# Half of a chunk's decay factors from stored rows instead of a matmul, in a one-core state-space kernel

## The reference, cut to what matters

```python
zxbcdt = hidden_states @ in_proj_w.T            # 1024 tokens, 512 -> 18560
xBC = silu(causal_conv4(zxbcdt[..., DIN:DIN + CONV_DIM]))   # x, B, C
dt = softplus(dt + dt_bias); Adt = -exp(A_log) * dt
L = exp(segment_sum(Adt))                       # exp of differences of running sums, 0 above the diagonal
Gm = einsum('bcihn,bcjhn->bhcij', C, B)
Y_diag = einsum('bhcij,bcjhd->bcihd', Gm * L, xs)
states = ...                                    # carried from chunk to chunk with exp(A_cumsum)
y = (Y_diag + Y_off + D * x) * silu(gate)
y = rmsnorm_by_group(y) * norm_w                # 8 groups of 1024 channels
x = x + y @ out_proj_w.T + ffn(layernorm(x))
```

## Time and profile before

| | |
|---|---|
| median of 3 runs | 1941.55 us (1940.65 to 1942.32) |
| profiled execution | 1946.74 us, span of its instructions 1945.0 us |
| mean granted clock of TensorE | 0.993 |
| PE / PEld busy | 97% / 76% of the span |
| DVE / ACT / POOL busy | 75% / 60% / 49% |
| cells with tiles | 60 of 64, mean length 25.8 us (328.86 to 1876.21 us) |

### The profile page before, as it was taken

How to read it: one execution, slowest core, us unless ns; L and a number is a source line. 1 busy time by engine, 2 the same in 40 slices (tenths; PEclk the granted TensorE clock), 3 DMA queues, 4 the chain that set the end, 5 groups by cost and what they waited for, 6 DMA issues and landing times.

```text
span 1945.0 us, 29309 instructions
## 1 busy us (share of the span) xinstructions
PE 1888.3 (97%) x10416; PEld 1478.3 (76%) x10416; DVE 1454.6 (75%) x1701; ACT 1169.6 (60%) x1908; POOL 951.2 (49%) x693
## 2 busy tenths in 40 slices
PE   7998999999999999999998999999999999999997
PEld 4776777777777777777776777878787878787875
DVE  6876645878787877778785878686878787877766
ACT  3334346767677776767676556566665656565643
POOL 6656643555555455555553444444344444444432
PEclk9999999999999999999999999999999999999998
DMA  2324463455454646464646353333424242424231
GB/s 88 119 82 141 137 218 93 134 164 181 148 188 135 210 131 225 136 213 128 208 131 222 86 153 128 114 110 95 146 77 155 83 161 82 156 77 150 77 115 44
DMA packets 123102, 264.62 MB, mean 136 GB/s; under 512 B 18112, under 2 KB 24384, under 8 KB 122704
## 3 DMA queue, kind: packets, MB, share of 16 engines
q1 hardware_dynamic: 88240, 161.55, 26.4%
q10 hardware_dynamic: 34720, 101.20, 16.2%
HBM read 216.82 MB, written 45.88 MB: 135 GB/s over the span
## 4 chain that ended last, share of the span: by engine, by line
PE 86%; issue 3%; POOL 3%; DVE 3%; DMA 3%; ACT 2%; ACTq 1%; SPq 0%; DVEq 0%; POOLq 0%
PE bank L1065 39%; PE bank L1123 6%; PE bank L1164 6%; PE bank L1185 5%; PE bank L1178 5%; PE bank L1098 5%; PE bank L1085 5%; PE bank L1130 3%; PE bank L721 3%; PE bank L694 3%; PE bank L1110 3%; PE bank L680 1%; DMA wlo_scratch<-stage 1%; POOL wxp L314 1%; DMA ecs<-ecs_scratch 1%
## 5 line engine op out<-in xcount | busy, mean ns | idle before, releaser
L1065 PE MATMUL bank<-xnp,wxp 128*128 128x512 f32 x3432 | 864.8, 404 | 11.3 <-POOL wxp L1443 6.4
L1065 PEld LDWEIGHTS bank<-xnp,wxp 128*128 128x128 f32 x3432 | 636.4, 189 | 164.0 <-POOL wxp L1443 16.6
L1443 POOL TENSOR_TENSOR wxp<-wxs,wxp 128x512 fp32r<-128x512 f32 x286 | 382.8, 1341 | 537.0 <-ACT wxp L1294 536.4
L1543 DVE SCALAR_TENSOR_TENSOR conv<-bank,cws,conv 128x509 f32<-128x509 f32 (+2 forms) x480 | 357.9, 746 | 11.3
L1301 ACT ACTIVATE conv<-bank,cbs,cws 128x512 f32<-128x512 f32 x160 | 124.2, 776 | 281.8 <-PE bank L1065 263.1
L1474 POOL TENSOR_TENSOR yl<-gT,yh 128x1024 fp32r<-128x1024 f32 x63 | 151.8, 2409 | 214.3 <-ACT yh L1359 214.3
L1294 ACT ACTIVATE wxp<-wxs 128x512 fp32r<-128x512 f32 x286 | 178.1, 623 | 0.7 <-DMA wxs<-wp 0.7
L1646 DVE SCALAR_TENSOR_TENSOR M<-M,gb 128x1024 f32<-128x1024 f32 x128 | 171.9, 1344 | 7.5 <-DVE gb L1638 0.5
L1345 ACT ACTIVATE ya<-xT,dch 128x128 f32<-128x128 f32 x512 | 156.1, 390 | 0.0
L1336 ACT ACTIVATE M<-bank 128x1024 f32<-128x1024 f32 x64 | 65.7, 1026 | 137.0 <-PE bank L1130 137.0
L1178 PE MATMUL bank<-wosh,yh 128*128 128x512 f32 x512 | 135.7, 407 | 5.1 <-issue 5.0
(11 more groups left out here) (166 smaller groups left out, 2847.0 us busy)
## 6 DMA issues: line engine op xcount, KB each, us to landing
wxs<-wp SPq DMA_DIRECT2D x288, 256.0 KB, 2.7
wosh<-whi_scratch ACTq DMA_DIRECT2D x64, 512.0 KB, 6.2
wosl<-wlo_scratch ACTq DMA_DIRECT2D x64, 512.0 KB, 11.2
ecs<-ecs_scratch ACTq DMA_DIRECT2D x112, 256.0 KB, 4.4
stage<-wout SPq DMA_DIRECT2D x64, 256.0 KB, 3.0
whi_scratch<-stagh SPq DMA_DIRECT2D x64, 256.0 KB, 2.0
wlo_scratch<-stage SPq DMA_DIRECT2D x64, 256.0 KB, 2.3
wxs<-w SPq DMA_DIRECT2D x56, 256.0 KB, 2.8
```

What stands on the lines that cost most here:

```text
L1065: last = pe.matmul(bank(k), wxp[:, k % 2, a, kk, :], xnp[:, b, kk, :], start=kk == 0 and a + b == 0, stop=kk == KT - 1 and a == 1)
L1443: pool.tensor_tensor(wxp[:, k % 2, 1], wxs[:, k % AHEAD], wxp[:, k % 2, 0], ALU.subtract).then_inc(w_lo, 1)
L1543: last = dve.scalar_tensor_tensor(out=conv[:, n % CB, back:], in0=bank(k)[:, 0:TH - back], scalar=cws[:, g, j, i:i + 1], in1=conv[:, n % C ...
```

## The change

The first 8 of a chunk's 16 heads no longer get their exponents from PE. The prologue stores the running sums as rows in DRAM (`rows_scratch`, one more transfer on ACT's queue, for which POOL waits before it overwrites the source), and a fourth table with -cs_j beside the three others. For every cell SP loads 8 rows of 128 sums, repeated over all partitions (512 KB written), into `M[:, 0:8]` once `diagonal` of the cell before is done (`load_sums`). A new DVE operation `bound(q+1)`, behind `scale_state(q+1)`, forms max(-cs_i, -cs_j) in place, which takes the mask's part. `exp_a` becomes eight activations of 128x128 with a bias per partition in place of one of 128x1024 from PSUM. `exp_b` stays as it was, from one pair of matmuls. `exp_a` moves on ACT from ahead of `high_y` to just ahead of `exp_b`; the `high` behind the z tile `ks[2]` moves ahead of the exps, while the emptying of `ks[2]` stays behind them. On DVE `sum_tiles(q)` now goes ahead of `weigh(q+1, 0)`. `segr` has 8 heads in place of 16.

```diff
+            def load_sums(q):
+
+                if q < CELLS:
+                    _, half, g, c = place(q)
+                    sp.wait_ge(yd_mm, done(q))
+                    sp.dma_start(M[:, 0:HB].rearrange("p h t -> p (h t)"),
+                                 bc(rows_dram[half * CH + c, g, 0:HB].rearrange("h i -> (h i)"), 0, [P, HB * P])
+                                 ).then_inc(d_m, 16)
...
                 diagonal(q)
-                if more:
-                    segment_a(q + 1)
                 for k in ks[2:3]:
                     project(k)
...
             def exp_a(q):
-                act.wait_ge(sa_mm, done(q + 1))
-                act.wait_ge(yd_mm, done(q))
-                act.activation(M[:, 0:HG // 2].rearrange("p h t -> p (h t)"), X[:], ACT.Exp).then_inc(e_a, 1)
+                u, _, _, c = place(q)
+                if c == 0:
+                    act.wait_ge(d_tab[u % 2], (u // 2 + 1) * 16 * (1 + PARTS))
+                act.wait_ge(m_min, done(q + 1))
+                for h in range(HB):
+                    last = act.activation(M[:, h], M[:, h], ACT.Exp, scale=-1.0, bias=tab[:, u % 2, 3, c, h:h + 1])
+                last.then_inc(e_a, 1)
...
                     refine(two[0])
-                if more:
-                    exp_a(q + 1)
                 high_y(q)
                 square(q)
                 if closes(q):
                     leave_bank(ks[2])
+                else:
+                    for k in ks[2:3]:
+                        high(k + 2)
                 if more:
+                    exp_a(q + 1)
                     exp_b(q + 1)
                 load_row(q + 2)
                 if not closes(q):
                     for k in ks[2:3]:
-                        leave_bank(k)
+                        empty_bank(k)
...
+            def bound(q):
+
+                u, _, _, c = place(q)
+                if c == 0:
+                    dve.wait_ge(d_tab[u % 2], (u // 2 + 1) * 16 * (1 + PARTS))
+                dve.wait_ge(d_m, 16 * (q + 1))
+                dve.scalar_tensor_tensor(out=M[:, 0:HB], in0=M[:, 0:HB], scalar=-1.0,
+                                         in1=bc(tab[:, u % 2, 3, c, 0:HB], 2, [P, HB, P]), op0=ALU.mult,
+                                         op1=ALU.max).then_inc(m_min, 1)
...
                     scale_state(q + 1)
+                    bound(q + 1)
                     take_gram(q + 1)
+                sum_tiles(q)
+                if more:
                     weigh(q + 1, 0)
-                sum_tiles(q)
```

More of the change, by code:

```diff
@@ L47 @@
 OUTW = 12
-TABS = 3
+TABS = 4
 CREDIT = 8
@@ L52 @@
 PAIRS = P // 2
+HB = HG // 2
 SEG = PAIRS + PARTS * HG
@@ L116, in build @@
         d_st = sem("d_st")
+        d_rows = sem("d_rows")
         banks = [pb(sets, f"bank{i}", [P, 1024]) for i in range(4)]
-        shared = (stage, stagh, wout, whi_dram, wlo_dram, xn_dram, d_raw, st_sc, st_hi, st_lo, d_st)
+        shared = (stage, stagh, wout, whi_dram, wlo_dram, xn_dram, d_raw, st_sc, st_hi, st_lo, d_st, rows_dram, d_rows)
         first = prologue(nc, sb, sem, banks, xnp, acc, ident, upper, epsc, hidden, wdt, dt_bias, a_log, c1, c2, w1, w2,
@@ L156, in prologue @@
              cws, cbs, nws, dch, d_const, d_saved, d_rest, left, w_hi, w_lo, t_mm, shared):
-    stage, stagh, wout, whi_dram, wlo_dram, xn_dram, d_raw, st_sc, st_hi, st_lo, d_st = shared
+    stage, stagh, wout, whi_dram, wlo_dram, xn_dram, d_raw, st_sc, st_hi, st_lo, d_st, rows_dram, d_rows = shared
     with ExitStack() as ctx:
@@ L389, in gpsimd @@
                     pool.wait_ge(s_seg, 1)
+                    pool.wait_ge(d_rows, 16)
                     pool.tensor_tensor(flat, flat, csb[:, 0], ALU.subtract).then_inc(s_seg, 1)
@@ L502, in scalar @@
                                            ACT.Exp).then_inc(s_ta, 1)
+                        act.activation(tabs[:, half, :, 3].rearrange("p g c h -> p c g h"),
+                                       cs[:, half * CH:(half + 1) * CH, :].rearrange("p c (g h) -> p c g h", g=G),
+                                       ACT.Copy, scale=-1.0).then_inc(s_ta, 1)
+                if n == PERM + 4:
+                    act.wait_ge(s_trc, NT // 2)
+                    act.dma_start(rows_dram.rearrange("c g h i -> (g h) c i"), csT[:]).then_inc(d_rows, 16)
                 if n == PERM + 8:
@@ L604, in steps_two @@
                     dt_half = dt[:, half * CH:(half + 1) * CH, :].rearrange("p c (g h) -> p c g h", g=G)
-                    dve.wait_ge(s_ta, 2 * half + 2)
+                    dve.wait_ge(s_ta, 3 * half + 3)
                     for c in range(CH):
@@ L860, in scan @@
         built = sem("built")
+        d_m, m_min = sem("d_m"), sem("m_min")
         tap_d, conv_step, conv_d, silu_d, z_d = (
             sem(x) for x in ("tap_d", "conv_step", "conv_d", "silu_d", "z_d"))
-        yo_mm, st_mm, xt_mm, yd_mm, sa_mm, sb_mm, g_mm, o_mm, q_mm = (
-            sem(x) for x in ("yo_mm", "st_mm", "xt_mm", "yd_mm", "sa_mm", "sb_mm", "g_mm", "o_mm", "q_mm"))
+        yo_mm, st_mm, xt_mm, yd_mm, sb_mm, g_mm, o_mm, q_mm = (
+            sem(x) for x in ("yo_mm", "st_mm", "xt_mm", "yd_mm", "sb_mm", "g_mm", "o_mm", "q_mm"))
         e_a, e_b, y_sq, y_hi, y_lo = (sem(x) for x in ("e_a", "e_b", "y_sq", "y_hi", "y_lo"))
@@ L1017, in sync @@
             load_tab(0)
+            sp.wait_ge(d_rows, 16)
+            load_sums(0)
             for k in range(AHEAD + 2, TILES + AHEAD + 2):
@@ L1036, in sync @@
                     load_tile(k + 2 + AHEAD)
+                    if i == 1:
+                        load_sums(q + 1)
                     if two and i == 1:
@@ L1043, in sync @@
                             fetch(slices(q + 1)[0])
+                if not tiles_of(q):
+                    load_sums(q + 1)
                 if q and (q - 1) // CH % G == G - 1:
@@ L1050, in tensor @@
         def tensor(pe):
-            for s in (yo_mm, st_mm, xt_mm, yd_mm, sa_mm, sb_mm, g_mm, o_mm, q_mm):
+            for s in (yo_mm, st_mm, xt_mm, yd_mm, sb_mm, g_mm, o_mm, q_mm):
                 pe.sem_inc(s, CREDIT)
@@ L1125, in diagonal, with segment_b @@
                 last.then_inc(yd_mm, 1)
-            def segment(q, n):
-                for b in range(2):
-                    head = n * (HG // 2) + b * (HG // 4)
-                    last = pe.matmul(X[:, b * 512:(b + 1) * 512], segl[:, q // CH % 2, q % CH],
-                                     segr[:, head:head + HG // 4, :].rearrange("p h t -> p (h t)"),
-                                     start=True, stop=True)
-                last.then_inc(sb_mm if n else sa_mm, 1)
-            def segment_a(q):
+            def segment_b(q):
                 u, _, _, c = place(q)
@@ L1141, in segment_a @@
                 pe.wait_ge(e_b, done(q))
-                segment(q, 0)
-            def segment_b(q):
-                pe.wait_ge(e_a, done(q + 1))
-                segment(q, 1)
+                for b in range(2):
+                    last = pe.matmul(X[:, b * 512:(b + 1) * 512], segl[:, q // CH % 2, q % CH],
+                                     segr[:, b * (HG // 4):(b + 1) * (HG // 4), :].rearrange("p h t -> p (h t)"),
+                                     start=True, stop=True)
+                last.then_inc(sb_mm, 1)
             def gram(q):
@@ L1309, in gate, with empty_bank @@
                 act.activation(gT[u % 2][:, j, :], bank(k), ACT.Silu).then_inc(z_d, 1)
-            def leave_bank(k):
+            def empty_bank(k):
                 if tile(k)[3] == "x":
@@ L1315, in leave_bank @@
                     gate(k)
+            def leave_bank(k):
+                empty_bank(k)
                 high(k + 2)
@@ L1329, in exp_a @@
             def exp_a(q):
-                act.wait_ge(sa_mm, done(q + 1))
-                act.wait_ge(yd_mm, done(q))
-                act.activation(M[:, 0:HG // 2].rearrange("p h t -> p (h t)"), X[:], ACT.Exp).then_inc(e_a, 1)
+                u, _, _, c = place(q)
[5 more added lines that the diff above has]
+                last.then_inc(e_a, 1)
             def exp_b(q):
                 act.wait_ge(sb_mm, done(q + 1))
+                act.wait_ge(yd_mm, done(q))
                 act.activation(M[:, HG // 2:].rearrange("p h t -> p (h t)"), X[:], ACT.Exp).then_inc(e_b, 1)
@@ L1523, in vector @@
         def vector(dve):
-            for s in (conv_step, conv_d, s_mul, s_add, u1_d, u3_d, y_d, x_dt, x_dec, g_cp, m_mul, y_s, r_v, acc_d):
+            for s in (conv_step, conv_d, s_mul, s_add, u1_d, u3_d, y_d, x_dt, x_dec, g_cp, m_min, m_mul, y_s, r_v, acc_d):
                 dve.sem_inc(s, CREDIT)
@@ L1671, in vector @@
                 convolve(k)
+                if k == 8:
+                    bound(0)
                 if k == 14:
```

11 lines of the change are left out of this document (5 added, 6 removed).

## The result

The changed kernel takes 2155.61 us (median; 2153.78 to 2156.1) against 1941.93 us for the kernel before in the same comparison: a ratio of 1.109, 95% interval 1.1077 to 1.1104. The forecast of slower was right; the time lies 5.6 us above the top of the range and 50.6 us above the number predicted. The profiled execution took 2156.1 us. Its span is 2154.4 us against 1945.0 before, so 209 us more, where the sum said 163.

What follows compares the result with a forecast made beforehand. PE, busy 97% of the span, was taken as the bound, with a later chain through DVE, ACT and POOL making it wait: 1946.7 + 163 = 2110, less 5.2 us to the median, so 2105 us; range 2035 to 2150.

Steps and rivals of the forecast that it cites:

- the sum: Whole kernel: 157 us more in 15 units, 3 in the last unit, 3 for start and prologue; 163 us in all.
- The chain through DVE, ACT and the banks: From E, the end of DVE's `gate(q)`: `bound` ends at E+7.2, tap of `ks[3]` starts at E+13.1, 5.3 us later.
- the lengths of places 1 and 2: E to E in a unit's second and third cells: 31.6 and 26.2 us in the first half, +5.0 and +2.7.
- PE merely waits longer: On PE, the removed matmuls' time turns into waiting, already counted in a unit's growth of 11.1 or 9.7 us.
- the prologue and tail: Outside the 15 units: 3 us for start and prologue, and 3 us for the last unit at 1 us a cell.
- Rival (b): DVE keeps the port for `bound`, chain 1.2 us shorter at three places of each unit, 54 us less: 2050; 17%.
- I take it as hidden: SP's 512 KB row load per cell: lands in 3.6 us, issued some 4 us ahead of E, wanted at E+4.8.
- the one ahead of `exp_a` is hidden, since it stands ahead of the wait: On ACT, of the 1.28 us table loads only the one behind `exp_b` counts in the chain.
- rival (c): PE's clock drops behind gaps: two losses a unit, 15 x 3.2 = 48 us, giving 2150; 20%.
- The main case: The longer chain through DVE, ACT and POOL makes PE wait: 2105 us, between 2075 and 2130; 50%.
- 0.24 us each, which makes 31 us: On PE, the worth of the 64 removed pairs of matmuls, by spacing: 31 us.
- rival (e): Faster: PE's 31 us from the removed matmuls are gained in full, 1911 us; 5%.

Runs made afterwards that it cites:

- rows_resident: The changed kernel with one head's row of sums loaded once and kept for `bound`, in place of the 64 loads per cell; 2111.93 us.
- table_hidden: The changed kernel without ACT's own wait for the tables ahead of `exp_a`, which leaves a single wait at every place; 2130.43 us.
- resident_and_table: The changed kernel with both the rows kept in SBUF and ACT's wait for the tables ahead of `exp_a` removed; 2092.91 us.
- bank_first: The changed kernel with ACT emptying `ks[2]` and `ks[3]` ahead of both exps, and DVE convolving `ks[3]` ahead of the first weighing; 2004.18 us.
- half left out: The kernel before without `segment_a` and `exp_a` and nothing in their place, the first half of `M` keeping a constant; 1927.14 us.

## Why the prediction missed its range though its chain held

**Right.** The chain through DVE, ACT and the banks (bound E+7.0, tap E+12.7) and the lengths of places 1 and 2 within 0.6 us; that PE merely waits longer instead of giving time back (though at place 0 for `add_out` and not, as the sum has it, 2.6 us for the convolution: the bank of `diagonal`, which it starts at 19.2, comes free with `add_out` at 21.4, and the same chain sets both); the prologue and tail (forecast 6 us; E of the first cell came 1.5 us later, the last two cells grew by 5.7 and the end by -0.7). Rival (b) is refuted: POOL's `low` took its turn between the two DVE operations, and it and `bound` were both stretched to 2.3 us, as in the earlier trace rows. The Trainium skill, "SBUF — State Buffer", on the two sides of the memory, has the loser of the shared pair wait for the whole instruction; the trace agrees, 2.30 us for `bound` behind POOL and 1.23 us at place 0, where the load had made it late and POOL was done.

**The step that failed: "I take it as hidden"**, of the row load. That was read from a load that lands in 3.6 us in its median; at place 0 it shares the DMA engines with the output weights and took 10.8 us. `rows_resident` brings place 0 to 28.2 and 28.6 (forecast 28.4) and place 3 of the first half to 27.9 (forecast 27.7). At place 3 the prediction saw the load as 2 us late and costed PE at nothing; it was 3.95 us late, and without `scale_state` there is nothing else in front of `bound`.

**The second: "the one ahead of `exp_a` is hidden, since it stands ahead of the wait".** True with one wait, not at place 3, where `exp_a` has two. It costs there 1.28 us on the chain; `table_hidden` brings place 3 of the second half from 32.3 to 30.2 (forecast 30.6). The prediction argued it from ACT's list at place 1 and let it stand for all places.

**Third, the size of rival (c).** The main case counted no clock loss. In the timeline of the kernel after (from 320 us on), of 156 rows of twelve matmuls 19 took over 3.4 us instead of 3.05, 26.9 us more in all, and of 56 rows of four matmuls of `into_state` (L1124) 13 took over 2.3 us instead of 1.9, 20.9 more: 32 slow stretches in 15 units, 48 us of PE's busy time. That is the two a unit that rival (c) assumed, with its 48 us, 2150. In the kernel before there was one such row in that time and no such group. The mean granted clock fell from 0.993 to 0.964: worked out from the two means, some 155 us of the span stood at the lower level, against 27. In the stretch at place 0 shown above the granted clock was 0.94 and then 0.90, so a part of it ran at the lower level of 1.2 GHz:

```profile
1034.00:1060.00 26.00, 23.07 (x127) 18.03 (x126) 17.48 (x20) 12.28 (x21) 8.42 (x6) 0.94 0.85 280
1060.00:1080.00 20.00, 19.21 (x107) 14.52 (x106) 16.73 (x22) 14.27 (x27) 12.09 (x13) 0.90 0.54 170
1080.00:1110.00 30.00, 25.72 (x146) 20.04 (x145) 23.31 (x26) 18.43 (x36) 13.48 (x10) 1.00 0.43 123
```

(start:end, length, busy us of PE, PEld, DVE, ACT and POOL, granted clock, DMA share, GB/s). But the loss isn't a cause of its own, and doesn't simply add: of the 13 slow groups 11 are at place 0, seven of them in the first half behind waits for `wosl` and the exps and four in the second behind waits for the sum of squares (L1688) and the exps, and `rows_resident` leaves 5 groups in all; of the 19 slow tiles 8 are at place 3, and `table_hidden` leaves one there. With both repairs 15 slow tiles and 5 groups remain, 23 us of busy time (ten of the tiles at place 1), and yet the lengths from E to E are close to those of the forecast without a clock. At place 1 the trace shows why. In units 0 to 6 of the changed kernel the fifth tile was slow in four and PE then waited 0.2 us for POOL's `low` ahead of the last tile; in the other three it was not slow and PE waited 1.7 us; the length was 30.7 to 31.8 us in the four and 30.8 to 32.0 in the three. There the loss is taken up in full by the wait that follows. How much of the 48 us lies on the path at the other places was not separated.

**Fourth, a term over-sized.** "0.24 us each, which makes 31 us": the upside of the removed matmuls was 17 us. It did not enter the main sum, but rival (e) should have read 1925, not 1911.

The sum: 15 units grew by 202.8 us (from 1547.9 to 1750.7 between the first and the 61st E) where the forecast had 157; the 46 us between are 29 us in the first eight units and 17 us in the next seven. `resident_and_table`, which has neither of the first two steps' failures, takes 2093 us against the 2105 forecast; that it is 12 us less was not followed up.

Where the expected gain went, as a ladder from that floor (in another sequence the steps weigh differently: without the new order the row load was worth 44 us, not 37): 1927 with half left out; 1946 with `bound` and one exp; 1965 with eight exps; 2002 with the row load; 2156 with the exps ahead of the emptying of the banks. The last rung, the largest, is the one that the order makes: 151 of its 153 us came with `bank_first` alone.

## What to carry to other kernels

Where an engine at 97% waits on others only through a double buffer, price a change by what it puts ahead of the instruction that frees the buffer: here an emptying that came 5 us late, with the losses to the clock that followed, cost nine times (151 us) the 17 us of matmuls that were saved. Take a load as hidden only after looking at what else the queues carry at each place of the loop, and a table load only after looking at the waits of its instruction at every place. Here the larger operations won on both engines: 1.06 us (without the bias) against 2.4 for the exps on ACT, 2.2 against 3.6 us for the bound on DVE, where each small operation could lose the port to POOL again.
